# Reading the moving operand of the expert products as pairs of columns 256 apart

## The reference, cut to what matters

```
x = x + layernorm(attention(layernorm(x)))     # linear attention, 4 heads of 32
x = x + layernorm(ffn(layernorm(x)))
# ffn: over all 8 experts, every token goes through each of them
for wg, wu, wd in experts:                     # 128x512, 128x512, 512x128
    h = silu(x @ wg) * (x @ wu)
    acc = acc + h @ wd
```

## Time and profile before

| | |
|---|---|
| median of 3 runs | 592.17 us (592.11 to 592.64) |
| the profiled execution | 592.38 us |
| its span | 590.6 us |
| granted TensorE clock, mean | 0.999 |
| PE busy | 583.5 us (99%) |
| DVE busy | 444.1 us (75%) |
| ACT busy | 349.3 us (59%) |
| POOL busy | 170.5 us (29%) |

### The profile page before, as it was taken

How to read it: one execution, slowest core, us unless ns; L and a number is a source line. 1 busy time by engine, 2 the same in 40 slices (tenths; PEclk the granted TensorE clock), 3 DMA queues, 4 the chain that set the end, 5 groups by cost and what they waited for, 6 DMA issues and landing times.

```text
span 590.6 us, 9218 instructions
## 1 busy us (share of the span) xinstructions
PE 583.5 (99%) x2633; PEld 463.3 (78%) x2633; DVE 444.1 (75%) x982; ACT 349.3 (59%) x626; POOL 170.5 (29%) x205
## 2 busy tenths in 40 slices
PE   9999999999999999999999999999999999999996
PEld 5677888788887888778888788878888788888885
DVE  5996886788767886779766887678876787668666
ACT  5778666555674555745557556654567545555554
POOL 4898680037000370015500353004600032001001
PEclk9999999999999999999999999999999999999999
DMA  5522110201101020100202002020110201010000
GB/s 164 152 82 89 36 36 1 73 19 42 49 36 37 19 67 25 59 30 1 89 0 72 18 19 71 1 72 19 37 37 0 73 19 36 1 37 18 2 0 19
DMA packets 28032, 24.46 MB, mean 41 GB/s; under 512 B 3024, under 2 KB 20944, under 8 KB 27984
## 3 DMA queue, kind: packets, MB, share of 16 engines
q1 hardware_dynamic: 27408, 23.73, 12.5%
q10 hardware_dynamic: 576, 0.20, 0.1%
HBM read 15.27 MB, written 8.65 MB: 41 GB/s over the span
## 4 chain that ended last, share of the span: by engine, by line
PE 96%; DVE 1%; ACT 1%; issue 1%; POOL 0%; POOLq 0%; DVEq 0%; ACTq 0%
PE gate_ps L1010 10%; PE gate_ps L1013 10%; PE gate_ps L1011 10%; PE up_ps L1010 10%; PE up_ps L1013 10%; PE acc_ps L1010 10%; PE acc_ps L1013 10%; PE up_ps L1011 10%; PE acc_ps L1011 10%; PE att_ps L1095 1%; PE att_ps L1106 1%; PE up_ps L1154 1%; PE att_ps L1068 0%; PE att_ps L1102 0%; PE att_ps L1011 0%
## 5 line engine op out<-in xcount | busy, mean ns | idle before, releaser
L604 ACT ACTIVATE gs<-gate_ps 128x512 f32<-128x512 f32 x255 | 152.6, 598 | 210.5 <-PE gate_ps L1013 209.2
L820 DVE TENSOR_TENSOR h<-gs,up_ps 128x512 f32<-128x512 f32 x255 | 174.4, 684 | 124.5 <-PE up_ps L1013 112.9
L807 DVE TENSOR_TENSOR h_lo<-h,h_hi 128x512 fp32r<-128x512 f32 x255 | 189.7, 744 | 0.8 <-ACT h_hi L581 0.7
L581 ACT ACTIVATE h_hi<-h 128x512 fp32r<-128x512 f32 x255 | 159.3, 625 | 11.8 <-DVE h L820 10.3
L1010 PE MATMUL gate_ps<-x1nT_hi,wg_hi 128*128 128x512 f32 (+1 forms) x256 | 104.3, 407 | 0.0
L1010 PE MATMUL up_ps<-x1nT_hi,wu_hi 128*128 128x512 f32 (+1 forms) x256 | 101.1, 395 | 0.0
L1013 PE MATMUL up_ps<-x1nT_lo,wu_hi 128*128 128x512 f32 (+1 forms) x256 | 101.0, 394 | 0.0
L1013 PE MATMUL gate_ps<-x1nT_lo,wg_hi 128*128 128x512 f32 (+1 forms) x256 | 100.9, 394 | 0.0
L1011 PE MATMUL gate_ps<-x1nT_hi,wg_lo 128*128 128x512 f32 (+1 forms) x256 | 100.7, 393 | 0.0
L1011 PE MATMUL up_ps<-x1nT_hi,wu_lo 128*128 128x512 f32 (+1 forms) x256 | 100.7, 393 | 0.0
L1010 PE MATMUL acc_ps<-h_hi,wd_hi 128*128 128x512 f32 x254 | 100.6, 396 | 0.0
(11 more groups left out here) (238 smaller groups left out, 504.0 us busy)
## 6 DMA issues: line engine op xcount, KB each, us to landing
w_raw<-in_L_ffn_Wg_dram SPq DMA_DIRECT2D x8, 256.0 KB, 2.9
w_raw<-in_L_ffn_Wu_dram SPq DMA_DIRECT2D x8, 256.0 KB, 2.8
w_raw<-in_L_ffn_Wd_dram SPq DMA_DIRECT2D x8, 256.0 KB, 3.2
x_in<-in_L_attn_x_dram SPq DMA_DIRECT2D x7, 256.0 KB, 2.7
t_dram_acc<-t_blk_acc SPq DMA_DIRECT2D x7, 256.0 KB, 2.3
t_out_acc<-t_dram_acc SPq DMA_DIRECT2D x28, 64.0 KB, 2.0
out_dram<-res SPq DMA_DIRECT2D x7, 256.0 KB, 2.0
t_dram_x<-t_blk_x SPq DMA_DIRECT2D x6, 256.0 KB, 2.1
```

What stands on the lines that cost most here:

```text
L581: act.activation(h_hi[s % NH][:, :], h[s % NGU][:, :], ACT.Copy).then_inc(s_hhi, 1)
L604: act.activation(gs[q][:, :], gate_ps[q][:, :], ACT.Silu).then_inc(s_silu, 1)
L807: dve.tensor_tensor(h_lo[s % NH][:, :], h[s % NGU][:, :], h_hi[s % NH][:, :].bitcast(F32), ALU.subtract).then_inc(s_hlo, 1)
L820: dve.tensor_tensor(h[q][:, :], gs[q][:, :], up_ps[q][:, :], ALU.mult).then_inc(s_h, 1)
```

## The change

1. All expert products (gate, up, down) read the moving operand through `pairs`: columns 0, 256, 1, 257, 2, 258 and so on. The output is written contiguously. So `h` and the accumulator hold the tokens in the order that follows from it; the down product applies the same reading again, and the accumulator ends with the four token blocks interleaved column by column.
2. To match, `x1nT` is laid out in blocks 0, 2, 1, 3 (`BLOCK`; GpSimd writes `x1n` in that order, ACT and DVE write the first batch so), DVE's transpose of `acc_ps` reads it with a step of four columns (`by_group_of_acc`), the final statistics take the blocks in that order, and the last accumulator is added with interleaved reads into `last_sum` (the buffer `xh`).
3. The tables are moved: on all engines, the attention's pieces from A on stand one step later.
4. Before the bodies, the last run of bf16 matmuls is 11 and 2 instead of 20, and between the two stand six fp32r matmuls of 512 columns on the first weights, two in each of three other reading orders.

```diff
-PE_AT = {"kT": 1, "A": 8, "M": 9, "G": 10, "attn": 11}
-DVE_AT = {"next_xnT_lo": 30, "kmax": 2, "acc": 2, "E_T": 3, "A": 9, "fin_stats": 9, "M": 10, "fin_scale": 11, "z": 12, "z_stats": 12,
-          "next_stats": 15, "x1_stats": 17, "x1n_T": 20, "next_T": 23, "x1n_lo": 26}
-ACT_AT = {"exp": 2, "G": 11, "x1n_hi": 25, "next_xnT": 28, "next_xnT_hi": 29}
-POOL_AT = {"yb": 4, "fin_rstd": 10, "fin_out": 12, "z_rstd": 13, "x1": 13, "x1_rstd": 17, "next_rstd": 20, "next_xn": 20}
-BUSY = {"start": 8, "w": 5, "attn": 20}
+PE_AT = {"kT": 1, "A": 9, "M": 10, "G": 11, "attn": 12}
+DVE_AT = {"next_xnT_lo": 31, "kmax": 2, "acc": 2, "E_T": 3, "A": 10, "fin_stats": 10, "M": 11, "fin_scale": 12, "z": 13, "z_stats": 13,
+          "next_stats": 16, "x1_stats": 18, "x1n_T": 21, "next_T": 24, "x1n_lo": 27}
+ACT_AT = {"exp": 2, "G": 12, "x1n_hi": 26, "next_xnT": 29, "next_xnT_hi": 30}
+POOL_AT = {"yb": 4, "fin_rstd": 11, "fin_out": 13, "z_rstd": 14, "x1": 14, "x1_rstd": 18, "next_rstd": 21, "next_xn": 21}
+BUSY = {"start": 8, "w": 5, "attn": 11, "end": 2}
+BLOCK = (0, 2, 1, 3)
+def pairs(v):
+    return v.rearrange("p (a b) -> p b a", a=2)
+def pairs_of(v, i):
+    return v.rearrange("p (a i b) -> p i b a", a=2, i=2)[:, i]
+def blocks_of(v, i):
+    return v.rearrange("p (a i b) -> p i a b", a=2, i=2)[:, i]
...
+        def by_group_of_acc(v):
+            return v.rearrange("p (i r k) -> p i k r", k=J, r=32)
...
-                    dve.transpose(grouped(t_blk["acc"][:, :]), by_group(acc_ps[:, :])).then_inc(s_acc, 1)
+                    dve.transpose(grouped(t_blk["acc"][:, :]), by_group_of_acc(acc_ps[:, :])).then_inc(s_acc, 1)
...
-                dve.tensor_tensor(accT[:, half], last_acc_ps[i][:, half], accT[:, half], ALU.add).then_inc(s_acc, 1)
+                dve.tensor_tensor(last_sum[:, i * JH:i * JH + JH, :].rearrange("p j t -> p t j"),
+                                  last_acc_ps[i][:, half].rearrange("p (t j) -> p t j", j=JH),
+                                  accT[:, :].rearrange("p (t j i) -> p i t j", j=JH, i=2)[:, i],
+                                  ALU.add).then_inc(s_acc, 1)
...
-                    products(ps[:, :], w_hi[k][:, e, cols], w_lo[k][:, e, cols], x1nT_hi[par][:, :],
-                             x1nT_lo[par][:, :], True, True, s_x1nT_lo, b + 1).then_inc(s_done, 1)
+                    products(ps[:, :], w_hi[k][:, e, cols], w_lo[k][:, e, cols], pairs(x1nT_hi[par][:, :]),
+                             pairs(x1nT_lo[par][:, :]), True, True, s_x1nT_lo, b + 1).then_inc(s_done, 1)
...
-                products(acc_ps[:, :], w_hi[2][:, e, cols], w_lo[2][:, e, cols], h_hi[q][:, :], h_lo[q][:, :],
+                products(acc_ps[:, :], w_hi[2][:, e, cols], w_lo[2][:, e, cols], pairs(h_hi[q][:, :]), pairs(h_lo[q][:, :]),
...
             keep_busy(BUSY["attn"])
+            pe.wait_ge(s_whi, 1)
+            w0, w1 = w_hi[0][:, 0, :], w_hi[0][:, 0, 0:P]
+            forms = [w0.rearrange("p (a b) -> p b a", a=4), w0.rearrange("p (a b) -> p b a", a=8),
+                     w0.rearrange("p (b a) -> p a b", a=2)]
+            for moving in forms:
+                for _ in range(2):
+                    pe.matmul(up_ps[0][:, :], w1, moving, start=True, stop=True)
+            keep_busy(BUSY["end"])
...
-                pe.transpose(last_banks[j][:, 0:P], accT[:, j * P:j * P + P], ident[:, :]).then_inc(s_last_T, 1)
+                pe.transpose(last_banks[j][:, 0:P], last_sum[:, j, :], ident[:, :]).then_inc(s_last_T, 1)
```

More of the change, by code:

```diff
@@ L33, with two @@
 FIRST_POOL = {"x_rstd": 3, "xn": 3, "yb": 9, "next_rstd": 15, "next_xn": 15, "z_rstd": 19, "x1": 19, "x1_rstd": 24}
-PE_AT = {"kT": 1, "A": 8, "M": 9, "G": 10, "attn": 11}
-DVE_AT = {"next_xnT_lo": 30, "kmax": 2, "acc": 2, "E_T": 3, "A": 9, "fin_stats": 9, "M": 10, "fin_scale": 11, "z": 12, "z_stats": 12,
-          "next_stats": 15, "x1_stats": 17, "x1n_T": 20, "next_T": 23, "x1n_lo": 26}
-ACT_AT = {"exp": 2, "G": 11, "x1n_hi": 25, "next_xnT": 28, "next_xnT_hi": 29}
-POOL_AT = {"yb": 4, "fin_rstd": 10, "fin_out": 12, "z_rstd": 13, "x1": 13, "x1_rstd": 17, "next_rstd": 20, "next_xn": 20}
-BUSY = {"start": 8, "w": 5, "attn": 20}
-FIRST = 2
+PE_AT = {"kT": 1, "A": 9, "M": 10, "G": 11, "attn": 12}
[4 more added lines that the diff above has]
+BUSY = {"start": 8, "w": 5, "attn": 11, "end": 2}
+FIRST = 2
+BLOCK = (0, 2, 1, 3)
[5 more added lines that the diff above has]
+    return v.rearrange("p (a i b) -> p i a b", a=2, i=2)[:, i]
+def two(v):
+    return v.rearrange("p (a b) -> p a b", a=2)
 def build(nc, x, gamma, beta, w_qkv, w_out, b_out, Wg, Wu, Wd, out):
@@ L162, in build @@
         last_acc_ps = [att_ps, gate_ps[(STEPS - 2) % NGU]]
+        last_sum = xh
         last_banks = [up_ps[(STEPS - 2) % NGU], last_gate_ps[0], last_up_ps[0], last_gate_ps[1]]
@@ L425, in power, with scale_of @@
                                    expo[:, 0:n * J].rearrange("p (a j) -> p a j", j=J), ALU.pow).then_inc(done, 1)
-            def scale_of(k, c, dst, src, done, which=0):
+            def scale_of(k, c, dst, src, done, which=0, place=range(J)):
                 wait_alone(pool, s_rstd[k], c)
@@ L430, in scale_of @@
                 for j in range(J):
-                    last = pool.tensor_scalar(dst[:, j, :], src[:, j, :], nm[k][:, j:j + 1],
+                    last = pool.tensor_scalar(dst[:, place[j], :], src[:, j, :], nm[k][:, j:j + 1],
                                               rstd[k][:, which, j:j + 1], ALU.add, ALU.mult)
@@ L459, in attention @@
                     power("x1", c, 1, s_rstd["x1"])
-                    scale_of("x1", c, x1n, x1[par], s_x1n)
+                    scale_of("x1", c, x1n, x1[par], s_x1n, place=BLOCK)
             def body(b, par, first, nxt, last):
@@ L665, in _ @@
             act.wait_ge(s_f_n, 1)
-            act.activation(x1nT_hi[0][:, HALF], att_ps[:, HALF], ACT.Copy).then_inc(s_f_hi, 1)
+            act.activation(blocks_of(x1nT_hi[0][:, :], 0), two(att_ps[:, HALF]), ACT.Copy).then_inc(s_f_hi, 1)
             act.wait_ge(s_f_n, 2)
-            act.activation(x1nT_hi[0][:, REST], up_ps[2][:, HALF], ACT.Copy).then_inc(s_x1nT_hi, 1)
+            act.activation(blocks_of(x1nT_hi[0][:, :], 1), two(up_ps[2][:, HALF]), ACT.Copy).then_inc(s_x1nT_hi, 1)
             bodies(act, body)
@@ L771, in finish @@
                     for j in range(J):
-                        last = dve.bn_stats(st["fin"][:, j, :], ffn[:, j])
+                        last = dve.bn_stats(st["fin"][:, j, :], ffn[:, BLOCK[j]])
                     last.then_inc(s_st["fin"], 1)
@@ L777, in finish @@
                     for j in range(J):
-                        last = dve.tensor_scalar(fn[:, j, :].rearrange("p (i r) -> p i r", r=32), ffn[:, j],
+                        last = dve.tensor_scalar(fn[:, j, :].rearrange("p (i r) -> p i r", r=32), ffn[:, BLOCK[j]],
                                                  mv["fin"][:, j, 0:1], rstd["fin"][:, 0, j:j + 1],
@@ L966, in _ @@
             dve.wait_ge(s_f_hi, 1)
-            dve.tensor_tensor(x1nT_lo[0][:, HALF], att_ps[:, HALF], x1nT_hi[0][:, HALF].bitcast(F32),
-                              ALU.subtract).then_inc(s_f_lo, 1)
+            dve.tensor_tensor(blocks_of(x1nT_lo[0][:, :], 0), two(att_ps[:, HALF]),
+                              blocks_of(x1nT_hi[0][:, :], 0).bitcast(F32), ALU.subtract).then_inc(s_f_lo, 1)
             dve.wait_ge(s_x1nT_hi, 1)
-            dve.tensor_tensor(x1nT_lo[0][:, REST], up_ps[2][:, HALF], x1nT_hi[0][:, REST].bitcast(F32),
-                              ALU.subtract).then_inc(s_x1nT_lo, 1)
+            dve.tensor_tensor(blocks_of(x1nT_lo[0][:, :], 1), two(up_ps[2][:, HALF]),
+                              blocks_of(x1nT_hi[0][:, :], 1).bitcast(F32), ALU.subtract).then_inc(s_x1nT_lo, 1)
             for j in range(J):
@@ L1028, in gate_up @@
                     for half, hi_made, lo_made in ((HALF, s_f_hi, s_f_lo), (REST, s_x1nT_hi, s_x1nT_lo)):
+                        x_h, x_l = (pairs_of(v[par][:, :], int(half is REST)) for v in (x1nT_hi, x1nT_lo))
                         pe.wait_ge(hi_made, 1)
                         for hi, lo, ps, _ in kinds:
-                            pe.matmul(ps[:, half], hi, x1nT_hi[par][:, half], start=True, stop=False)
-                            pe.matmul(ps[:, half], lo, x1nT_hi[par][:, half], start=False, stop=False)
+                            pe.matmul(ps[:, half], hi, x_h, start=True, stop=False)
+                            pe.matmul(ps[:, half], lo, x_h, start=False, stop=False)
                         pe.wait_ge(lo_made, 1)
                         for hi, _, ps, done in kinds:
-                            last = pe.matmul(ps[:, half], hi, x1nT_lo[par][:, half], start=False, stop=True)
+                            last = pe.matmul(ps[:, half], hi, x_l, start=False, stop=True)
                             if half is REST:
@@ L1121, in last_step @@
                         pe.wait_ge(s_free, t - 3 + 1 + i)
```

(4 more changed lines are left out.)

## The result

The changed kernel takes 555.87 us (median of 4 runs, 555.68 to 556.11) against 592.20 us: ratio 0.9385, 95% interval 0.9369 to 0.9402, 36.3 us faster. The forecast was 563 with a range of 551 to 596; so the direction and the range held, but the time is nearer to the first rival (554) and lies under the forecast's own narrower range, 561 to 568.

What follows compares the result with a forecast made beforehand. PE's pace on 2286 matmuls, 233.3 ns each, was taken as the bound, 90% of the span. The terms summed as 592.38 - 30.5 - 0.2 + 1.0 + 0.3 = 563.0, given as 563 us, range 551 to 596.

Steps and rivals of the forecast that it cites:

- the first rival: Pace of the main matmuls: all of the distance to bf16 (215.8 ns) goes, total 554 us; chance 0.22.
- Term 1: 2286 matmuls read in pairs: 220.0 ns each, gain 30.5 us; bounds a gain of 40.0 and a loss of 445.
- from two sizes to a slope and a constant: fp32r matmuls of 512 and 256 columns, 560 and 288 cycles: 1.0625 cycles a column, 16 cycles fixed.
- My own sign for a wrong slope: Last gate and up: 256-column halves will not move by half of what the 512-column matmuls move.
- Terms 2 and 7: DVE's step-of-four accumulator transpose: no change, 2.5 us if doubled; two interleaved last additions: 0.3 us, bounds 0 to 0.8.
- Term 3: Stalls over the eight bodies, PE waiting behind ACT's exponential with its table loads: 1.0 us, bounds 0 and 3.
- Term 4: Tables one step later from A on: the later place keeps the margin of E's fixed-time loads; cost nil.
- Term 6: Warm-up: 20 bf16 matmuls become 13, six fp32r added at 0.22 or 0.428 us each; loss 0 to 0.7 us, taken 0.
- The slower rival: Main matmuls: alternating places makes the fetch pay, pace over 233.3 ns; 1037 us at two cycles a column; chance 0.20.

## Why the prediction was right, and where it was not

**What bounds it.** Right: PE's pace on 2286 matmuls. Contiguous reading put back takes the time to 591.97, all else kept.

**Term 1, the pace.** The mechanism was right as far as it went (a loss that only fp32r has, and that the reading order removes; that it is one of fetching stays a reading), its size was not. I took 220.0 ns and a gain of 30.5 us; the pace is 215.7 ns and the gain 2286 x 17.6 = 40.2 us. The step that failed is the one from two sizes to a slope and a constant: "a column costs 1.0625 cycles, one lost in 16 columns, and 16 cycles stay fixed". What fails is the fixed part. Pairs take 389 cycles at 384 columns and 518 at 512, 5 and 6 over one cycle a column, where I had 16. Whether the loss itself goes with the columns stays open: it is 40 cycles at 384 and 42 at 512, but the start alone moves the contiguous pace by up to 8 ns (19 cycles). My own sign for a wrong slope did not appear, since the 256-column halves moved by 8.3 ns, about half of 17.6; yet pairs stand there at the floor of 112 ns, so it could not tell. It was the first rival that happened, and the bf16 rows were the better guide to what remains. The Trainium skill's columns over the clock plus 2.5 ns ("TensorE: Matmul & The Clock Gate", Back-to-back issue gap), which it gives for a matmul by itself and without naming a type, is 215.8 ns and agrees with pairs of fp32r too (215.7), not with contiguous fp32r (233.3).

**Terms 2 and 7, DVE's strided reads.** Transpose 713 ns, as taken; the ground given for it was weak, since it compared the lengths of PE's records, which say little of a pace, and on another engine. The two additions add 0.2 us each; with one of them before the first transpose, some 0.2 us on the path against 0.3 taken.

**Term 3, what is late next.** Sum too small, place wrong. I put 1.0 us on stalls, behind ACT's table loads. The added pauses are 3.2 us, and none stands there: they are at M_sb, at the accumulator's transpose, at Ek, at x1n and at `h_lo`, where a wait stood in the waits of before already, except for x1n. That the first body has less margin was right: half of the 3.2 us is there. Reading that list for small waits that would grow would have named the other four.

**Term 4, the tables.** Nil, as taken, and the reason given (E's way through DRAM has a fixed time, so the later place is needed) is borne out by the old tables: with them E's loads come late and the time is 2.6 us longer.

**Term 6, the warm-up.** The six matmuls took 443 ns on average, a little over the upper bound of 428, and no loss is to be seen behind them.

**The sum.** 592.38 - 40.2 - 0.2 + 3.2 + 0.2 = 555.4 against a profiled 555.68: 0.3 us are not assigned, and the pace's last digit is worth as much (most groups of pairs stand at 215.9 ns, which makes the gain 39.8). Forecast and result differ by 9.7 us from the pace, less 2.2 from the stalls: two misses of opposite sign, of which the second hid a part of the first.

**The slower rival.** It did not come true for fp32r, but its mechanism is real for the other types: bf16 in pairs 485 ns, plain float32 406 against 322. The Trainium skill's note on cachelines ("SBUF — State Buffer", under Door 1), two hits in succession or a penalty, agrees in direction with these and with eight places in turn (489 ns). Two hits are not enough here, though: bf16 in runs of 2 and 4 still takes 272 and 227 ns against 216. And it differs from fp32r in pairs, where no column follows another of its line and the pace is the best of all (215.7). The measurement decides.

## What to carry to other kernels

If matmuls in fp32r bound a kernel and follow one another at 233 ns per 512 columns, let the moving operand be read in pairs of columns at least 4 apart; pairs within each eight columns are enough for the pace, so the permutation can stay local. Undoing the permutation over all 512 columns cost nothing in DVE's transpose (713 ns either way) and 0.2 us in each of the last two additions; undoing the local one was not run. Do it for fp32r alone: with pairs half the operand apart bf16 pays 2.2 times and plain float32 1.26 times (bf16 in pairs 4 apart keeps its 216 ns and gains nothing; plain float32 was not tried so). When a pace changes by 8%, take the list of waits of before and retime each of its small entries; here that was worth 2.6 us and then 2.4 more.

## What the runs showed that I had not expected

- Distance is irrelevant from 4 columns (16 bytes) up: 215.7 to 216.4 ns at 4, 8, 16, 32, 64, 128, 256, 257, 258, 259, 260, 264 and 512 columns apart; 231 at 2.
- Of the numbers of places tried two is the best: one 233 ns, two 216, four 268 to 279, eight 489.
- Runs are worse than single columns for fp32r (330, 252, 241 ns for runs of 2, 4, 16 from two places), while bf16 is the other way round (272, 227, 216 for 2, 4, 8, and 485 for single columns).
- The contiguous pace depends on the start, 228 to 236 ns over starts 1 to 16 columns further, without an order that I can name. What the 42 cycles are remains open: the runs exclude a price that grows with the load of the weights, and fit a loss between successive columns of one 16-byte block, no more.
